# Reordering the first attention batches and transposing expert tokens in fp32r

## The reference

```
x = x + xattn(layernorm(x), ctx)      # 16 heads of 32, causal, softmax over keys
x = x + ffn(layernorm(x))
xattn: q = h @ Wq.T ; k, v = split(ctx @ Wkv_expand.T) ; softmax(q k / sqrt(32)) v ; @ Wout.T
ffn:   logits = h @ gate.T ; top 2 of 8 experts, weighted by their softmax
       expert: silu(gate) * up (352 wide), then down ; plus a shared expert 704 wide
```

## Time and profile before

| what | us |
|---|---|
| median of the timed runs | 361.02 |
| profiled execution, its own time | 359.25 |
| its span | 357.5 |
| TensorE busy (share of the span) | 339.3 (95%) |
| ScalarE busy | 232.2 (65%) |
| VectorE busy | 253.3 (71%) |
| GpSimd busy | 99.0 (28%) |

### The profile page before, as it was taken

One profiled execution on the slowest core, in us unless ns is written; L12 is line 12 of the kernel. 1 busy time (PEld: TensorE's weight loads), 2 busy tenths in 40 slices (PEclk: granted clock), 3 DMA queues, 4 the chain that ended last, 5 costly groups with the idle time before them and its releaser, 6 DMA issues.

```text
span 357.5 us, 6944 instructions
## 1 busy us (share of the span) xinstructions
PE 339.3 (95%) x2262; PEld 281.6 (79%) x2263; DVE 253.3 (71%) x464; ACT 232.2 (65%) x610; POOL 99.0 (28%) x115
## 2 busy tenths in 40 slices
PE   8997997999999998999999899999999999999992
PEld 7996785777776877889898788788878888887771
DVE  5776858999956248855577897877787878778810
ACT  4547979999973242213225588788878887888721
POOL 4256142555551000165300011122113211311131
PEclk9999999999999999999999999999999999999998
DMA  8999000000001789994599825434443444354233
GB/s 258 366 360 380 24 3 2 3 2 0 4 2 54 300 272 373 425 343 158 192 313 216 277 88 87 88 60 67 82 88 59 71 81 84 60 77 82 48 44 47
DMA packets 28667, 49.47 MB, mean 138 GB/s; under 512 B 6752, under 2 KB 11872, under 8 KB 27616
## 3 DMA queue, kind: packets, MB, share of 16 engines
q1 hardware_dynamic: 24496, 39.91, 34.3%
q0 software_dynamic: 4144, 9.23, 14.8%
HBM read 32.22 MB, written 16.92 MB: 137 GB/s over the span
## 4 chain that ended last, share of the span: by engine, by line
PE 74%; ACT 14%; DMA 4%; DVE 3%; issue 3%; POOLq 1%; POOL 0%; SPq 0%; ACTq 0%
PE bank L500 31%; PE bank L796 22%; ACT prob L918 10%; PE bank L811 9%; DMA out<-y_sb,dest 3%; PE bank L702 3%; PE bank L583 2%; PE bank L835 2%; PE bank L674 2%; ACT probT L873 2%; PE bank L492 1%; DMA w_sg<-sguT 1%; PE bank L688 1%; ACT w_sg_hi L873 1%; PE bank L555 1%
## 5 line engine op out<-in xcount | busy, mean ns | idle before, releaser
L1155 DVE TENSOR_TENSOR gu_parts<-w_gu,gu_parts 128x704 fp32r<-128x704 f32 x84 | 72.8, 888 | 21.2 <-ACT gu_parts L873 19.7
L873 ACT ACTIVATE gu_parts<-w_gu 128x704 fp32r x84 | 66.1, 790 | 15.7 <-PE bank L796 15.3
L481 POOL DMA_INDIRECT out<-y_sb,dest x21 | 33.1, 1577 | 145.8 <-ACT y_sb L1076 137.7
L796 PE MATMUL bank<-gu_parts,xsT_hi 128*128 128x352 f32 x336 | 69.8, 329 | 1.2 <-issue 1.2
L796 PEld LDWEIGHTS bank<-gu_parts,xsT_hi 128*128 128x128 f32 x336 | 55.2, 189 | 2.3 <-issue 2.3
L796 PE MATMUL bank<-gu_parts,xsT_lo 128*128 128x352 f32 x168 | 40.7, 323 | 0.0
L811 PE MATMUL bank<-w_dn,actT_plain 128*128 (+1 forms) x80 | 37.7, 592 | 0.0
L500 PE MATMUL bank<-x2T_hi,w_sg_lo 128*128 128x512 f32 (+1 forms) x88 | 32.2, 366 | 0.1
L500 PE MATMUL bank<-x2T_hi,w_sg_hi 128*128 128x512 f32 (+1 forms) x88 | 32.0, 363 | 0.0
L500 PE MATMUL bank<-x2T_lo,w_sg_hi 128*128 128x512 f32 (+1 forms) x88 | 31.9, 363 | 0.0
L873 ACT ACTIVATE act_s_hi<-act_s 128x512 fp32r<-128x512 f32 (+1 forms) x10 | 5.8, 579 | 36.6 <-DVE act_s L1338 28.4
(11 more groups left out here) (197 smaller groups left out, 779.0 us busy)
## 6 DMA issues: line engine op xcount, KB each, us to landing
w_gu<-guT SPq DMA_DIRECT2D x8, 1408.0 KB, 9.6
xs_dram<-xs_in SPq DMA_DIRECT2D x1, 5460.0 KB, 19.8
xs_in<-xs_dram SPq DMA_DIRECT2D x21, 256.0 KB, 2.6
w_dn<-dnT SPq DMA_DIRECT2D x8, 512.0 KB, 6.2
w_sg<-sguT SPq DMA_DIRECT2D x10, 256.0 KB, 5.7
w_dn<-dnT SPq DMA_DIRECT2D x8, 192.0 KB, 6.9
w_sd<-sdnT SPq DMA_DIRECT2D x5, 256.0 KB, 5.3
out<-xres SPq DMA_DIRECT2D x1, 1280.0 KB, 5.1
```

The lines of the kernel that those rows point to most:

```text
L481: pool.indirect_dma_start(out=out[:, :], out_offset=bass.IndirectOffsetOnAxis(ap=dest[:, i, 0:1], axis=0), in_=y_sb[i % 2][:, :], in_offse ...
L796: ins = pe.matmul(dst[:, 0:F], xsT[x_][:, c, :], gu2[w_][:, c, f0:f0 + F], start=c == 0 and n == 0, stop=c == C - 1 and n == 2)
L873: act.activation(dst, src, ACT.Copy).then_inc(s[sem], 1)
L1155: dve.tensor_tensor(lo_, src, hi_.bitcast(F32), ALU.subtract).then_inc(s[sem], 1)
```

## The change

It has three parts.

- Order in the first batches. Tile 1's transpose goes ahead of the last key product; the second filler runs 3 times, not 6. Transposes of tiles 2 and 3 are both put behind the third part of the query products, and those of tiles 5 and 6 both ahead of the last query group. A second projection `q_proj(1, 1)` goes ahead of the second scores, into bank B. Batch 0 then has pair 2 and the key of pair 1, and batch 1 only pair 3. The copies on ScalarE and VectorE follow.
- The first shared weights are split in the projection phase. GpSimd starts on the output weights after the first of these splits is complete, and takes their low parts after batch 0's normalisations. `no_row` gets a place of its own, the statistics of the first norm another one.
- The tokens of the expert loop are transposed as fp32r, against an fp32r copy of the identity which VectorE makes once.

```
 pool:
-            pool.wait_ge(s["xn"], NX)
+            pool.wait_ge(s["wsd_lo"], 1)
             (high parts of w_o, as before; low parts now in a helper)
+                if n == 0:
+                    for c in range(C):
+                        wo_lo(c)
 tensor:
             for j in range(C):
+                if j == C - 1:
+                    t1(1, S[1])
                 k_proj(0, j, bank[4 + j])
-            t1(1, S[1])
-            keep_busy(S[2:4], 6)
+            keep_busy(S[2:4], 3)
-                if c in (1, 2):
-                    t1(c + 1, S[c + 1])
+                if c == 2:
+                    t1(2, S[2])
+                    t1(3, S[3])
-                if j >= 1:
-                    t1(BLK + j - 1, S[j - 1])
+                if j == 1:
+                    t1(4, S[0])
+                if j == 2:
+                    t1(5, S[1])
+                    t1(6, S[2])
             k_proj(1, 0, CC)
             q_proj(1, 0, D)
+            q_proj(1, 1, B)
-            (fill(j): q_proj(1, j, D), k_proj(1, j, CC); j = 1 at b 0 r 2, 2 at b 1, 3 at b 1 r 2)
+                if b == 0:
+                    pe.wait_ge(s["KT"], C + 1)
+                    k_proj(1, 1, CC)
                 for r in range(R):
+                    if r == 1 and b == 0:
+                        pe.wait_ge(s["QT"], C + 2)
+                    if r == 2 and b == 0:
+                        q_proj(1, 2, D)
+                        pe.wait_ge(s["KT"], C + 2)
+                        k_proj(1, 2, CC)
+                    if r == 2 and b == 1:
+                        pe.wait_ge(s["QT"], C + 3)
+                        q_proj(1, 3, D)
+                        (waits for KT C + 3, oT_hi 1, oT_lo 1)
+                        k_proj(1, 3, CC)
-                pe.wait_ge(s["KT"], C + 2 if b == 0 else C * NBLK)
+                pe.wait_ge(s["KT"], C + 3 if b == 0 else C * NBLK)
             def t_x(i):
+                pe.wait_ge(s["idf"], 1)
-                    ins = pe.transpose(S[2][:, c * P:(c + 1) * P], xs_in[:, c * P:(c + 1) * P], ident[:, :])
+                    ins = pe.transpose(S[2][:, c * P:(c + 1) * P].bitcast(F32R),
+                                       xs_in[:, c * P:(c + 1) * P].bitcast(F32R), ident_f[:, :])
 scalar:
             wq_hi(0)
+            put_xnT(1, S[1])
+            wq_hi(1)
             put_kT(0, 2, bank[6])
-            put_xnT(1, S[1])
             put_kT(0, 3, bank[7])
             (then wq_hi 2, 3, put_xnT 2, 3)
                 put_qT(0, j, bank[4 + j])
+                if j == 0:
+                    sg_hi(0)
+                if j == 1:
+                    put_xnT(4, S[0])
+                    sd_hi(0)
-                if b == 1:
-                    put_qT(1, 2, D)
+                (the same after exps(1, 0), at b == 0)
                 if b == 1:
                     put_qT(1, 3, D)
-                    sg_hi(0)
-                    sd_hi(0)
 vector:
             (put_qT reads bank B; statistics of tile 2 behind wq_lo(1), not ahead of wq_lo(0))
+            dve.tensor_copy(ident_f[:, :], ident[:, :]).then_inc(s["idf"], 1)
+            apply1(6)
             xnT_lo(4, S[0])
-            apply1(6)
+            sg_lo(0)
             xnT_lo(5, S[1])
             xnT_lo(6, S[2])
+            sd_lo(0)
             for r in range(R - 1):
                 normalised(0, r)
+            put_qT(1)
             (at b == 0: put_kT(1) between masked(1, 2) and masked(1, 3), put_kT(2) after them)
                     put_v(b + 1)
-                    if b == 1:
-                        sg_lo(0)
-                        sd_lo(0)
```

More of the change, by code:

```diff
@@ L109, in build @@
         silu_s[t] = m.inside(cursor, f"silu_s{t}", [P, WX[t]])
+    act_p_at = small[0]
     act_p = m.inside(small, "act_p", [P, T], F32R)
@@ L173, in build @@
     xs_in = sb("xs_in", [P, XW])
-    no_row = xs_in
+    no_row = nc.alloc_sbuf_tensor_at("no_row", [P, XW], F32, offset=act_p_at)
+    ident_f = sb("ident_f", [P, P], F32R)
     negmax = sb("negmax", [SQ, R, C])
@@ L177, in build @@
     rrow = sb("rrow", [SQ, R, C])
-    bn1, mv1, var1, rstd1 = (sb(n, [P, NX, k]) for n, k in (("bn1", 6), ("mv1", 2), ("var1", 1), ("rstd1", 1)))
+    bn1, mv1, var1, rstd1 = (m.inside(score_at, n, [P, NX, k]) for n, k in (("bn1", 6), ("mv1", 2), ("var1", 1), ("rstd1", 1)))
     bn2, mv2, var2, rstd2 = (sb(n, [P, NX, k]) for n, k in (("bn2", 6), ("mv2", 2), ("var2", 1), ("rstd2", 1)))
@@ L230, in build @@
         "x0 xt1 xt2 xrest wq0 wq1 wq2 wq3 wkeys wvals wo wgate ctx0 ctx1 wsg0 wsg1 wsd0 wsd1 wsd2 we we_late "
-        "const zt sel zero "
+        "const zt sel zero idf "
         "ctx_hi ctx_lo wkv_hi wkv_lo wq_hi wq_lo wo_hi wo_lo wg_hi wg_lo wsg_hi wsg_lo wsd_hi wsd_lo "
@@ L418, in _, with wo_lo @@
                 pool.tensor_copy(w_o2[0][:, c, :], w_o[:, c, :]).then_inc(s["wo_hi"], 1)
-            for c in range(C):
+            def wo_lo(c):
                 pool.wait_ge(s["wo_hi"], c + 1)
@@ L646, in _ @@
                     shared_gu(0, 0, (0,))
-                if b == 1:
-                    fill(2)
+                if b == 0:
+                    pe.wait_ge(s["KT"], C + 1)
+                    k_proj(1, 1, CC)
                 for r in range(R):
-                    if r == 2 and b <= 1:
-                        fill((1, 3)[b])
+                    if r == 1 and b == 0:
[7 more added lines that the diff above has]
+                        q_proj(1, 3, D)
+                        pe.wait_ge(s["KT"], C + 3)
+                        pe.wait_ge(s["oT_hi"], 1)
+                        pe.wait_ge(s["oT_lo"], 1)
+                        k_proj(1, 3, CC)
                     if r == 1 and b >= 2:
@@ L950, in _ @@
             wq_hi(0)
+            put_xnT(1, S[1])
+            wq_hi(1)
             put_kT(0, 2, bank[6])
-            put_xnT(1, S[1])
             put_kT(0, 3, bank[7])
-            for c in range(1, C):
-                wq_hi(c)
+            wq_hi(2)
+            wq_hi(3)
             put_xnT(2, S[2])
+            put_xnT(3, S[3])
             wkv_hi("wvals", slice(H, 2 * H))
-            put_xnT(3, S[3])
             ctx_hi(1)
@@ L961, in _ @@
                 put_qT(0, j, bank[4 + j])
-                if j >= 1:
-                    put_xnT(BLK + j - 1, S[j - 1])
+                if j == 0:
[3 more added lines that the diff above has]
+                    sd_hi(0)
+                if j == 2:
+                    put_xnT(5, S[1])
+                    put_xnT(6, S[2])
             put_v(0)
@@ L981, in _ @@
                     exps(b + 1, 0)
+                if b == 0:
+                    put_qT(1, 2, D)
                 if b >= 3:
@@ L1215, in put_qT @@
                 dve.wait_ge(s["Q"], C + j + 1)
-                dve.tensor_scalar(qT[:, j, XC[1]], D[:, 0:WX[1]], SCALE, None, ALU.mult).then_inc(s["QT"], 1)
+                dve.tensor_scalar(qT[:, j, XC[1]], B[:, 0:WX[1]], SCALE, None, ALU.mult).then_inc(s["QT"], 1)
             def put_kT(j):
@@ L1257, in _ @@
             apply1(1)
-            dve.wait_ge(s["xt2"], 16)
-            stats1(2)
             wq_lo(0)
@@ L1262, in _ @@
             wq_lo(1)
+            dve.wait_ge(s["xt2"], 16)
+            stats1(2)
+            wq_lo(2)
             stats1(3)
             apply1(2)
-            wq_lo(2)
+            wq_lo(3)
             apply1(3)
-            wq_lo(3)
             xnT_lo(2, S[2])
             xnT_lo(3, S[3])
+            dve.tensor_copy(ident_f[:, :], ident[:, :]).then_inc(s["idf"], 1)
             dve.wait_ge(s["xrest"], 16)
@@ L1293, in _ @@
                     x2T_lo(b - 3, CC)
+                if b == 0:
+                    put_kT(1)
                 if b + 1 < NB:
@@ L1296, in _ @@
                 if b == 0:
-                    put_qT(1)
-                if b <= 1:
-                    put_kT(b + 1)
+                    put_kT(2)
                 if b == 2:
```

## The result

The changed kernel takes 354.83 us (median of 4 runs, 353.98 to 355.46), the kernel before in the same comparison 361.06 (360.21 to 361.37): ratio 0.9852, 95% interval 0.9823 to 0.988. A second comparison gave 355.10 against 360.26, ratio 0.985 (0.9818 to 0.9881). So the gain is 6.2 us by the first and 5.2 by the second. The profiled execution took 355.46, 3.8 less than the profiled one of before.

What follows compares the result with a forecast made beforehand. ScalarE was taken to pace steady attention, TensorE the projections and expert loop. The front's 3.4 plus 2.0 for transposes made 5.4 us, from a median of 361.02 to 355.6 (chance 0.54); range 353.2 to 358.4.

Steps and rivals of the forecast that it cites:

- Projection phase: Up to the first scores: tile reordering starts them at 27.55, not 28.06, a net 0.5 us, bounds 0 and 1.1.
- the shared split puts VectorE in its place: Before the first scores: TensorE's 0.81 us wait for tile 6 goes, but VectorE's moved weight split then sets the start.
- Batches 0 and 1: Attention's first batches: 1.46 us of splits leave ScalarE and its idle time falls from 2.95 to 1.55 us.
- The front's 3.4: Projections through batch 2's third head group: 3.4 us gained, including 0.5 before the first scores; bounds 1.0 and 4.6.
- Rival 3: Before batch 2: the shared split fully delays first scores and ScalarE waits longer; 3.0 us gained, 358.0; chance 0.08.
- GpSimd's cover: Output-weight splits on GpSimd fit before normalisations need it; without that slack batch 1's transposes come up to 2 us late.
- Transposes: Expert loop: fp32r token transposes save 0.1 us a tile over 20 tiles, 2.0 us; bounds 0 and 3.7.
- The price of 0.085: Expert loop: us per fp32r token transpose, the middle between 0.064 and 0.110.
- rival 1: Expert loop: transposes at 0.064 us, on a line through fp32r products of 256 and 352 columns; 7.1 gained, 353.9; chance 0.20.
- Rival 2: Expert loop: fp32r transposes no faster, 0.110 us each, so only the front counts; 357.6; chance 0.13.
- Rival 4: Expert loop: short fp32r work falls to full fp32 product pace, 0.215 us per 128 columns; 366.0, slower by 5; chance 0.05.
- So the load allows it: Expert loop: loading 128 columns of weights would not stop fp32r token transposes from reaching 0.064 us.

Runs made afterwards that it cites:

- front alone: The changed kernel with the expert loop's token transposes back in fp32: 356.84 us, ratio 0.9896 to the kernel before.

## Why the prediction was right
**The sum.** Predicted were 355.6 and 5.4 us. By stages, the front takes off 0.4 (first scores, on average of the profiles with the new projection phase against those with the old), 1.0 and 1.6, the loop 1.94: 4.96. The timed runs say 5.2 and 6.2. The range held the time, and the case was the forecast, not a rival. The two profiled executions give 3.8: 0.53, 1.01, 1.61 and 1.94 less 1.03 of the third column (81.45 and 82.48) and 0.27 behind the last token transpose. That the timed medians of before stand at 361.06 and 360.26 with the same kernel explains most of the other difference. The profiled execution itself was forecast at 353.85 and took 355.46. The forecast had carried its distance of 1.77 from the median over as if it belonged to the kernel; 81.45 is at the low end of the third column's 81.43 to 83.00, so about 1 of it was that stage's luck in one execution.

**Projection phase: nearly right in size, wrong in the reason.** 0.5 us was forecast with first scores at 27.55. The first profile after has 27.53, the second 27.93, with 28.06 and 28.02 before. Counted from ScalarE's first key copy, which takes out when the execution got going, it is 19.65 before and 19.27 after in both: 0.4. The step "the shared split puts VectorE in its place" holds in that profile and yet decides nothing: with the split out of the way the first scores came 0.03 earlier. I had TensorE's value products end near 27.1 and their last record ends at 27.34, since the last normalisation waits for GpSimd and the last query group stands behind its transposes:
```profile
23.95 0.55 DVE L1170 TENSOR_SCALAR xn<-xres,mv,rstd 128x512 f32<-128x512 f32 x1 [0.51 <-POOL rstd L410]
...
24.97 0.36 PE L506 MATMUL bank<-xnT_hi,w_q_lo 128*128 128x256 f32 x1
```

**Batches 0 and 1: right, step by step, but for one wait.** Second scores 34.0 (33.97), third 42.8 (42.95), third head group of batch 2 51.67 (51.89), ScalarE's new waits 0.4, 0.2, 0.6 and 0.35 (0.39, 0.17, 0.51 and 0.78). The last was mis-sized: batch 1's last transposes come at 48.33, since the pair of projections starts when the second head group is transposed, and that waits for VectorE at 45.1. The front's 3.4 measures 3.0 by stages and 3.4 by the medians of the timed front alone (3.7 by its ratio). Rival 3, the front eaten down to 1.0, did not come.

**GpSimd's cover.** "Costs nothing as long as its cover holds" came out right, but for its own queue only. That its two-input work stops VectorE for 2.0 us was not in the sum. It cost nothing because VectorE had a gap there.

**Transposes: right in sum, in part by luck.** 2.0 us was forecast and 1.94 measured. The price of 0.085 was a choice, the middle between 0.064 and 0.110, and an added transpose measures 0.081. But 4 x 0.025 = 0.1 us a tile treats the set as if nothing but its own pace changed. The stretch with the set gives back 0.069 a tile, 1.4 us over 20 tiles, since 0.04 is lost at the border to the products; the other 0.03 a tile, 0.6 us, comes from the faster pace of the gate/up products in every second tile, which the sum didn't have. Taken apart, the term was 0.6 us too large, and an effect that the sum did not have filled it. The straight line of rival 1 appears in the first two gaps of a set (0.062 and 0.064) and doesn't last. Rival 2 fell with the period. Rival 4, the pace of a full fp32 product below 256 columns, did not come: no sign of a fall in pace.

"So the load allows it", drawn from transposes with 8 moving columns 0.066 apart, doesn't carry over to these. Behind the first one the weight loads of a set follow each other at 0.082 to 0.087 us in fp32r and 0.107 to 0.110 in fp32, which is also the pace of the transposes from the third gap on; whether load or transpose sets that pace no run shows. The Trainium skill ("TensorE: Matmul & The Clock Gate", LDWEIGHTS, loading the stationary operand) would have P/1.2 ns, by estimate 107 ns for 128 columns. The loads in fp32 agree with it, at 107 to 110 ns; those in fp32r, at 82 to 87 ns, don't, so it doesn't hold for them.

## What to carry to other kernels
Before moving work between stages, add up the critical engine's own queue between two fixed points: its idle time, what leaves, and what new waits come. That sum held within 0.4 us here (3.4 forecast, 3.0 by stages). Fill a wait of TensorE before a stage with independent products from a stage where another engine waits for TensorE, and take one-time preparation off the engine that sets the pace, into a stage where it has gaps. When an engine is named as releaser with a wait of 0.2 us, ask who is next: removing it gained 0.03. And compare by stages, since two profiled executions of one kernel differed by 1.03 us in a single stage, a fifth of the whole gain. In a loop go one step further and cut the period at fixed starts: here nearly a third of what the token transposes seemed to gain came from products that the change doesn't touch.

## What the hardware showed unasked
- A VectorE operation with both inputs in SBUF was held by GpSimd's with both inputs in SBUF: it took 2.65 us in place of 0.62 while GpSimd had four of the second kind queued (37.76 to 42.77), and ended 0.48 after the last of them, though one of the four ended and the next began in between. With two queued it ended 0.49 after them (0.89 us). VectorE's operations with an input in PSUM went on in 0.6 us beside them (row additions and copies from 37.87 to 39.86), and so did row maxima with one input in SBUF.
- fp32r transposes of 128 x 128: the first two gaps of a set are 0.060 to 0.065, the following 0.080 to 0.089; fp32: 0.107 to 0.110 throughout. The first product behind a set starts 0.080 to 0.088 after the last transpose in fp32r, and 0.028 or 0.029 after it in fp32.
- The same 24 gate/up products have two paces at a granted clock of 1.00: from the first to the fourth low-part pair 2.85 or 2.91 us. The loop's period is constant at 7.060 (fp32 sets of four) and 6.847 (all seven transposes in fp32r), alternates between 6.928 and 6.992 (tokens in fp32r), and repeats 7.423, 7.502 and 7.489 with eight fp32 transposes.
